# Preparing the next image six units before the last one ends, and the offset convolution in three parts

## The chip, the core and the metric

The program runs on one core of a Trainium2 chip. The metric is the device time of one execution in microseconds; the kernel before takes 4003.83 us (median of 3 runs, 3988.3 to 4007.59). It works on TensorE (PE), VectorE (DVE), ScalarE (ACT), GpSimd (POOL) and on DMA queues that SyncE (SP) and POOL feed.

## The reference, cut to what matters

The input x is [32, 192, 32, 32]. Two residual blocks follow each other, image by image, except for the last normalization, whose statistics run over the whole batch:

```
x = x + attention(group_norm(x))            # channel attention, 4 matmul stages
x = x + deform_block(group_norm(x))

deform_block(v):
    offset = clip(conv3x3(v, off_w) + off_b, -8, 8)         # 18 channels: y and x shift of 9 taps
    mask   = 2 * sigmoid(conv3x3(v, mask_w) + mask_b)       # 9 channels
    y      = sum over taps of w_tap . bilinear(v, position + tap + offset) * mask  + proj_b
    yn     = (y - mean) * rsqrt(var + 1e-5) * gamma + beta  # mean, var over batch and pixels
    return gelu(yn)
```

The 27 channels of offset and mask are computed together: this is the *offset convolution*.

## The kernel before, in words

Each of the 32 images is 8 tiles of 128 pixels. The sampling is done with matmuls: `Z = x2 . w` is computed per chunk of 4 rows (`zps`, split in two halves of 16 bits each, `zh` and `zl`), and for each tile a sparse matrix S of interpolation weights is built, turned and split in the same way (`sT`, `sps`, `sh`, `sl`), and then y = sum S . Z (`acc`). An image is 48 **units**. The main work of unit u, in `part1`, is:

- PE: `turn_s(u+2)` (three transposes, L666), `convolve(u)` (nine matmuls, L683 to L685), `z_group(u+10)` (five matmuls, L652 to L656). For the last units, u+2 and u+10 reach into the next image.
- ACT: the 16-bit copies `sh` of unit u+2 (L905) and `zh` of unit u+10 (L871). In each sixth unit it also takes y out of `acc` (`ypm`, L927 and L928).
- DVE: the remainders `sl` (L1161) and `zl` (L1155) behind them.
- POOL: one product `sT` (L1343) of row weights `ay` and column weights `bx` for two units, in a ring of three. So product p waits until PE has turned unit 2(p-3)+1.

PE may turn s of unit u+2 and convolve unit u only when DVE has written `sl` of unit u.

Beside this, `part0(k)` prepares the next image in 48 **steps** k, one behind the main work of each unit, and on every engine in the program's order (there is no planner; each engine is a straight list of instructions with waits on semaphores). Before the change step k stands in unit k of the image ahead. The steps that matter here:

- k = 0 to 4: statistics of x for the first group norm (DVE L993 to L1012, PE L517), k = 6 to 9: ACT normalizes, k = 12 to 22: attention (PE), k = 23 to 26: its result is added, k = 28: second group norm.
- k = 30 to 33: ACT normalizes into `x2`. k = 32 to 36: DVE writes the remainder (L1018) and, in `move`, two shifted copies (L1024, L1025) and two seam copies (L1027, L1028) of each of three planes. The last one raises `x2_moved`.
- k = 38 and 39: PE does the offset convolution, 4 tiles of 27 matmuls in each step (L594). It waits for `x2_moved`.
- k = 40 to 46: DVE takes the offsets out of PSUM (L1115 to L1122), makes the row weights in two halves (L1126, mask L1135, product L1137, which raises `hats`), ACT applies Abs and Relu to them, POOL and ACT make the column weights `bx` in four parts (L1327, L862 and L864). The first part belongs to step 41. The other three belong to main units (POOL after products 1, 4 and 10; ACT in units 4, 16 and 28).

Some work is tied to the unit, not to the step: PE turns the finished y (`turn_y`, L696) in units 14, 26, 38 and at the end, DVE scales it (`scale_y`, L1223) in units 19, 31, 43 and at the end, and DVE takes statistics of y in units 38, 39 and, for the second half, in units 5 and 6 of the next image (L1233). `z_group(0)` of the next image stands in unit 38 and waits for `x2_moved`.

```
part1(0, 0, True)
with nc.Fori(1, NB - 2, 2, ...) as b:
    part1(b, 1, True)
    part1(b + 1, 0, True)
part1(NB - 1, (NB - 1) % 2, False)
```

Two images are one round of a loop; the first and the last image stand outside it. Before image 0 the 48 steps of its own preparation run alone. `where_far`, at the end of every image, is a branch that skips a rare long pass.

Of the kernel before, what the change touches and what calls it, by code (L numbers as in the profile page):

```python
# [43 lines left out]
TILES = N // P  # L44
# [5 lines left out]
WRAP = 3  # L50
KO = 3 * C
UNITS = 6 * TILES
HEAD_SCALE = float((C // 4) ** (-0.5))
GN_EPS = 1e-5
BN_EPS = 1e-5
# [27 lines left out]
def build(nc, x, w_qkT, w_v, w_outT, b_out, w_off, b_off, w_proj, proj_b, gamma, beta,  # L83
          avg, cy, cx, eye, out):
    NB = x.shape[0]
# [4 lines left out]
    with ExitStack() as ctx:  # L90
# [154 lines left out]
        s_lo = sem("s_lo")  # L245
# [29 lines left out]

        SLOTS = UNITS
        CONST_DMAS = 4
# [58 lines left out]
        def images(program, eng):  # L336

            part0, part1, weights_ready = program  # L340
            for u in range(SLOTS):
                part0(u, 0, 0)
                if u == 15:
                    weights_ready()
            part1(0, 0, True)
            with nc.Fori(1, NB - 2, 2, engines=bass.OrderedEngineSet([eng.engine]), hint_back_edge=True) as b:
                part1(b, 1, True)
                part1(b + 1, 0, True)
            part1(NB - 1, (NB - 1) % 2, False)


        far_bodies = []
# [146 lines left out]
        def _(pe):  # L499
# [106 lines left out]
            def part0(u, b, par):  # L606
# [22 lines left out]
                    apply_m(u - 23, b)  # L629
                if u == 28:  # L630
                    group_stats(1, b)
                if 38 <= u < 40:
                    for t in range(TILES // 2):
                        offset_conv(TILES // 2 * (u - 38) + t, b, par)

            def z_group(g, b, par):

# [60 lines left out]
                mm.then_inc(yt_ps, 1)  # L698

            def far_pass(b, par, more):  # L700
                pe.wait_ge(s_lo, UNITS * (b + 1) + 2 * more)
                pe.wait_ge(y_ch, 4 * (b + 1))
                pe.wait_ge(y_pm, TILES * (b + 1))

# [39 lines left out]
            def part1(b, par, more):  # L744
# [5 lines left out]
                for u in range(UNITS):  # L750
                    if u + 2 < UNITS:
                        turn_s(u + 2, b)
                    elif more:
                        turn_s(u + 2 - UNITS, b + 1)
                    convolve(u, b, par)
                    if u == 9:
                        offset_max(b)
                    if u == 20:
                        flag = is_far(pe, b, par)
                    if u + AHEAD < UNITS:  # L760
                        z_group(u + AHEAD, b, par)
                    elif more:
                        z_group(u + AHEAD - UNITS, b + 1, 1 - par)
                    if u % 12 == 2 and u > 12:
                        turn_y(u // 12 - 1, b)
                    if more:
                        part0(u, b + 1, 1 - par)
                turn_y(3, b)
                where_far(flag, pe, b, par, more, far_pass, (fz_ps, FAR_Z), (fs_ps, FAR_UNITS), (fsz_done, FAR_UNITS),
                          (fyt_ps, TILES))  # L770
# [7 lines left out]
        def _(act):  # L778
# [128 lines left out]
            def part1(b, par, more):  # L907
# [5 lines left out]
                for u in range(UNITS):  # L913
# [8 lines left out]
                    if u % 6 == 5:  # L922
                        t = u // 6
# [6 lines left out]
                        split_z(u + AHEAD, b, par)  # L930
                    elif more:
                        split_z(u + AHEAD - UNITS, b + 1, 1 - par)
                    if more:
                        part0(u, b + 1, 1 - par)
                where_far(flag, act, b, par, more, far_pass, (fz_hi, FAR_Z), (fs_hi, FAR_UNITS), (fy_pm, TILES))

            images((part0, part1, lambda: None), act)
# [16 lines left out]
        def _(dve):  # L954
# [282 lines left out]
            def part1(b, par, more):  # L1237
# [5 lines left out]
                for u in range(UNITS):  # L1243
# [17 lines left out]
                        y_stats(u - 38, b, par)  # L1261
                    if u % 12 == 7 and u > 12:
                        scale_y(u // 12 - 1, b, par)
                    if more:
                        part0(u, b + 1, 1 - par)
                scale_y(3, b, par)
                where_far(flag, dve, b, par, more, far_pass, (fz_lo, FAR_Z), (f_st, 3 * TILES), (fs_lo, FAR_UNITS),
                          (fy_ch, TILES))
# [29 lines left out]
        def _(pool):  # L1298
# [14 lines left out]
                pool.tensor_tensor(nbias[:, :], nbias[:, :], minus[:, :], ALU.mult).then_inc(gn_bias, 1)  # L1313

            def part0(u, b, par):
                if u == 5:
                    group_rstd(0, b)
                if u == 29:
                    group_rstd(1, b)
                if u == 41:  # L1320
                    column_distance(0, b, par)

            def column_distance(q, b, par):
# [7 lines left out]
            def part1(b, par, more):  # L1331
                for p in range(3 * TILES):
                    t, ky = tile_at(p // 3, par), p % 3
# [10 lines left out]
                        .then_inc(st_made, 1)  # L1344
                    if p in (1, 4, 10):
                        column_distance((1, 4, 10).index(p) + 1, b, par)
                    if more:

                        for u in (2 * p - 4, 2 * p - 3):
                            part0(u, b + 1, 1 - par)  # L1350

            images((part0, part1, lambda: None), pool)

# [56 lines left out]
```

## Time and profile before

| | |
|---|---|
| median of 3 runs | 4003.83 us |
| the profiled execution: its time, its span | 3993.97 us, 3992.2 us |
| PE, DVE, ACT, POOL busy | 89%, 66%, 53%, 35% of the span |
| mean granted TensorE clock | 0.968 of full speed |
| two images in the middle of the run (rows below) | 230.65 us, 115.3 us each |

The span has three parts: about 120 us in which image 0 is prepared, 32 images, and about 200 us at the end in which PE is idle and the batch normalization is applied to y as it comes back from memory. A timeline row gives start and duration in us, the engine, the line, what is written and read, the shapes, and in brackets how long the engine was idle just before and which instruction ended that.

### The profile page before, as it was taken

The page shows a single profiled execution, that of the slowest core. Times are in us where ns is not written, and L with a number is a line of the kernel's source. Part 1 is how long each engine was busy: PE and PEld are TensorE (multiplying, and loading weights), DVE is VectorE, ACT ScalarE, POOL GpSimd, SP SyncE. Part 2 cuts the span into 40 slices and gives each one's busy share as a digit, 9 for nine tenths or more (in the row PEclk, how much of TensorE's full clock was granted, in tenths as well). Part 3 has the DMA queues.
Part 4 walks back from the last instruction along what each step waited for, and adds up shares of the span by engine and source line. Part 5 has one row for each costly group of instructions (what it writes and reads, how often), then busy time and mean ns, then how long its engine had stood idle before and what let it go on. Part 6 is the DMA issues. An engine that isn't in the chain of part 4 may idle for free.

```text
span 3992.2 us, 110012 instructions
## 1 busy us (share of the span) xinstructions
PE 3544.1 (89%) x38338; PEld 3034.8 (76%) x38338; DVE 2646.4 (66%) x5834; ACT 2111.3 (53%) x4790; POOL 1412.8 (35%) x1165
## 2 busy tenths in 40 slices
PE   3999999999999999999999999999999999999700
PEld 2788887888888888888888888888888888888700
DVE  3577766676677667677766676677667667766522
ACT  1555555565555555555555565555555555555432
POOL 1333333343433333333333343333333333333311
PEclk8999999999999999999999999999999999999955
DMA  2000000000000010000000000000000001000299
GB/s 63 20 10 28 28 27 22 28 28 19 20 28 28 20 28 28 28 10 28 28 20 28 28 28 15 23 28 28 20 28 28 28 10 28 28 20 18 76 377 322
DMA packets 50722, 170.05 MB, mean 43 GB/s; under 512 B 9664, under 2 KB 10880, under 8 KB 50176
## 3 DMA queue, kind: packets, MB, share of 16 engines
q1 hardware_dynamic: 39584, 136.75, 11.2%
q0 software_dynamic: 7168, 25.17, 1.6%
q8 instruction: 337, 5.52, 0.6%
q14 instruction: 209, 1.71, 0.1%
q10 hardware_dynamic: 3424, 0.90, 0.1%
HBM read 87.29 MB, written 75.50 MB: 41 GB/s over the span
## 4 chain that ended last, share of the span: by engine, by line
PE 66%; DVE 12%; issue 9%; DMA 4%; POOL 3%; ACT 3%; DVEq 1%; SPq 1%; ACTq 0%; POOLq 0%
PE sps L666 10%; PE acc L683 6%; PE acc L685 6%; PE acc L684 6%; PE l L594 4%; PE zps L652 3%; PE zps L656 3%; PE zps L653 3%; PE zps L655 3%; PE zps L654 3%; DVE zl L1155 3%; DMA xn<-x_scratch 2%; POOL sT L1343 2%; DVE sl L1161 2%; PE l L526 2%
## 5 line engine op out<-in xcount | busy, mean ns | idle before, releaser
L1343 POOL TENSOR_TENSOR sT<-ay,bx 128x768 f32<-128x768 f32 x768 | 1149.5, 1507 | 1363.4 <-PE sps L666 1292.5
L1161 DVE TENSOR_TENSOR sl<-sps,sh 128x384 f16<-128x384 f32 x1536 | 846.0, 551 | 563.8 <-ACT sh L905 557.7
L683 PE MATMUL acc<-zh,sh 128*128 128x192 f16 x4608 | 1133.7, 246 | 0.9 <-issue 0.6
L685 PE MATMUL acc<-zh,sl 128*128 128x192 f16 x4608 | 1133.6, 246 | 0.0
L684 PE MATMUL acc<-zl,sh 128*128 128x192 f16 x4608 | 1133.6, 246 | 0.0
L905 ACT CAST sh<-sps 128x384 f16<-128x384 f32 x1536 | 741.7, 483 | 695.3 <-PE sps L666 689.6
L871 ACT CAST zh<-zps 128x288 f16<-128x288 f32 x1536 | 620.4, 404 | 638.8 <-PE zps L656 611.7
L1155 DVE TENSOR_TENSOR zl<-zps,zh 128x288 f16<-128x288 f32 x1536 | 693.2, 451 | 334.3 <-ACT zh L871 325.4
L666 PE MATMUL sps<-eye,sT 128*128 128x128 f32 x4608 | 785.8, 279 | 127.2 <-DVE sl L1161 99.4
L666 PEld LDWEIGHTS sps<-eye,sT 128*128 128x128 f32 x4608 | 530.9, 140 | 283.5 <-DVE sl L1161 167.9
L684 PEld LDWEIGHTS acc<-zl,sh 128*128 128x128 f16 x4608 | 450.9, 98 | 17.7 <-issue 0.8
L683 PEld LDWEIGHTS acc<-zh,sh 128*128 128x128 f16 x4608 | 450.8, 98 | 2.4 <-DVE sl L1161 0.5
L685 PEld LDWEIGHTS acc<-zh,sl 128*128 128x128 f16 x4608 | 450.9, 98 | 0.0
L652 PE MATMUL zps<-wpr_h,x_hi_a 128*128 128x288 f16 x1344 | 384.6, 286 | 1.0 <-DVE zl L1155 0.6
L653 PE MATMUL zps<-wpr_l,x_hi_a 128*128 128x288 f16 x1344 | 384.4, 286 | 0.0
L654 PE MATMUL zps<-wpr_h,x_lo_a 128*128 128x288 f16 x1344 | 384.4, 286 | 0.0
L655 PE MATMUL zps<-wpr_h,x_hilo_b 128*128 128x288 f16 x1344 | 384.4, 286 | 0.0
L656 PE MATMUL zps<-wpr_l,x_hilo_b 128*128 128x288 f16 x1344 | 384.4, 286 | 0.0
L1327 POOL TENSOR_TENSOR bx<-off,cx_sb 128x576 f32<-128x576 f32 x128 | 155.5, 1215 | 459.0 <-DVE off L1122 459.0
L1309 POOL TENSOR_TENSOR rstd<-gvar,mhalf 128x2 f32<-128x2 f32 x64 | 44.9, 702 | 553.9 <-DVE gvar L1012 553.9
L594 PE MATMUL l<-wof,x2s_hi_a 128*128 128x54 f16 x1536 | 182.8, 186 | 9.8 <-DVE x2w_hilo_b L1028 9.8
L594 PE MATMUL l<-wof,x2s_lo_a 128*128 128x54 f16 x1536 | 182.6, 186 | 0.0
(200 smaller groups left out, 6482.7 us busy)
## 6 DMA issues: line engine op xcount, KB each, us to landing
xin<-in_x SPq DMA_DIRECT2D x32, 512.0 KB, 5.4
xin<-in_x SPq DMA_DIRECT2D x64, 256.0 KB, 6.0
x_scratch<-x SPq DMA_DIRECT2D x32, 512.0 KB, 2.7
y_scratch<-ych SPq DMA_DIRECT2D x32, 512.0 KB, 2.7
zh<-y_scratch SPq DMA_DIRECT2D x20, 512.0 KB, 11.1
zl<-x_scratch SPq DMA_DIRECT2D x20, 512.0 KB, 12.5
out<-zh POOLq DMA_DIRECT2D x20, 512.0 KB, 8.6
x_scratch<-x SPq DMA_DIRECT2D x32, 256.0 KB, 3.4
```

The lines of the kernel that those rows point to most:

```text
L594: mm = pe.matmul(o, src[:, row * W:(row + ROWS_T) * W], wof[:, m, k].rearrange("p i j -> p (i j)"), start=(k == 0 and n == 0), stop=(k == ...
L652: pe.matmul(o, at(0), wpr_h[:, 0, ky, n], start=True, stop=False)
L653: pe.matmul(o, at(0), wpr_l[:, 0, ky, n], start=False, stop=False)
L666: mm = pe.transpose(sps[u % 2][:, kx * P:(kx + 1) * P], sT[:, g, kx, c * P:(c + 1) * P], eye32[:, :])
L683: pe.matmul(acc[:, 0:C], s_h, zh[:, j, ky, z], start=start and kx == 0, stop=False)
L684: pe.matmul(acc[:, 0:C], s_h, zl[:, j, ky, z], start=False, stop=False)
L685: mm = pe.matmul(acc[:, 0:C], s_l, zh[:, j, ky, z], start=False, stop=stop and kx == 2)
L871: act.copy(z_piece(zh, g, par), zps[:, g % 2, 0:KO // 2]).then_inc(z_hi, 1)
L905: act.copy(sh[:, u % S_RING].rearrange("p k n -> p (k n)"), sps[u % 2][:, 0:3 * P]).then_inc(s_hi, 1)
L1155: dve.tensor_tensor(z_piece(zl, g, par), zps[:, g % 2, 0:KO // 2], z_piece(zh, g, par), ALU.subtract)\
L1161: dve.tensor_tensor(one(sl), sps[u % 2][:, 0:3 * P], one(sh), ALU.subtract).then_inc(s_lo, 1)
L1343: pool.tensor_tensor(sT[:, p % ST_RING].rearrange("p k (r x) -> p k r x", r=R), a, x_, ALU.mult)\
```

## The change

Every engine's step k + 6 now stands in unit k. In units 42 to 47 of image b stand steps 0 to 5 of image b + 2, since steps 6 to 47 of image b + 1 are done by then. Before image 0 these six steps of image 1 run too. Three images instead of one are written out behind the loop. On POOL the numbers of the steps change (5, 29, 41 become 9, 33, 45) because its loop over products now asks for units 2p and 2p+1 instead of 2p-4 and 2p-3; the same operations move by the same six units, three products. The offset convolution is done in steps 37, 38 and 39 with 2, 3 and 3 tiles.

```
+SHIFT = 6
...
+            for u in range(SHIFT):
+                part0(u, 1, 1)
+            part1(0, 0, 2)
+            with nc.Fori(1, NB - 4, 2, engines=bass.OrderedEngineSet([eng.engine]), hint_back_edge=True) as b:
+                part1(b, 1, 2)
+                part1(b + 1, 0, 2)
+            for b in range(NB - 3, NB):
+                part1(b, b % 2, min(2, NB - 1 - b))
+
+        def prepare(part0, u, b, par, more):
+
+            if u + SHIFT < SLOTS:
+                if more:
+                    part0(u + SHIFT, b + 1, 1 - par)
+            elif more == 2:
+                part0(u + SHIFT - SLOTS, b + 2, par)
...
-                if 38 <= u < 40:
-                    for t in range(TILES // 2):
-                        offset_conv(TILES // 2 * (u - 38) + t, b, par)
+                if 37 <= u < 40:
+                    for t in ((0, 1), (2, 3, 4), (5, 6, 7))[u - 37]:
+                        offset_conv(t, b, par)
...
-                    if more:
-                        part0(u, b + 1, 1 - par)
+                    prepare(part0, u, b, par, more)
...
-                    if more:
-
-                        for u in (2 * p - 4, 2 * p - 3):
-                            part0(u, b + 1, 1 - par)
+                    for u in (2 * p, 2 * p + 1):
+                        prepare(part0, u, b, par, more)
```

The change moves instructions in three places that the prediction speaks of. The first is PE where the offset convolution begins. Before, it stands in unit 38, behind a z product that itself waits for `x2_moved`, and behind the turn of y:

```order
L652 MATMUL zps<-wpr_h,x_hi_a 128x288 [waits z_lo,x2_moved]
L653 MATMUL zps<-wpr_l,x_hi_a 128x288
L654 MATMUL zps<-wpr_h,x_lo_a 128x288
L655 MATMUL zps<-wpr_h,x_hilo_b 128x288
L656 MATMUL zps<-wpr_l,x_hilo_b 128x288
L696 MATMUL yt<-eye,ypm 128x128 [waits y_ch,y_pm]
L697 MATMUL yt<-eye,ypm 128x128
L696 MATMUL yt<-eye,ypm 128x128
L697 MATMUL yt<-eye,ypm 128x128
L594 MATMUL l_1<-wof,x2s_hi_a 128x54 [waits x2_moved]
```

With the change it begins one step earlier, directly behind the z product of that unit (the lines of the new file are higher by some):

```order
L697 MATMUL acc<-zh,sl 128x192
L664 MATMUL zps<-wpr_h,x_hi_a 128x288 [waits z_lo]
L665 MATMUL zps<-wpr_l,x_hi_a 128x288
L666 MATMUL zps<-wpr_h,x_lo_a 128x288
L667 MATMUL zps<-wpr_h,x_hilo_b 128x288
L668 MATMUL zps<-wpr_l,x_hilo_b 128x288
L606 MATMUL l_1<-wof,x2s_hi_a 128x54 [waits x2_moved]
```

The z product ahead no longer waits for `x2_moved`, and the turn of y has gone from there to another step.

The second place is DVE behind the first half of the row weights (mask and product). Before:

```order
L1135 TENSOR_SCALAR mask<-mask 128x72
L1137 TENSOR_TENSOR ay<-ay,mask 128x288
L1159 ISA
L1161 TENSOR_TENSOR sl<-sps,sh 128x384 [waits s_hi]
L1154 ISA
L1155 TENSOR_TENSOR zl<-zps,zh 128x288 [waits z_hi]
L1218 ISA
L1223 TENSOR_SCALAR ych<-yt,unscale,pb 128x256 [waits yt_ps]
```

With the change:

```order
L1145 TENSOR_SCALAR mask<-mask 128x72
L1147 TENSOR_TENSOR ay<-ay,mask 128x288
L1169 ISA
L1171 TENSOR_TENSOR sl<-sps,sh 128x384 [waits s_hi]
L1164 ISA
L1165 TENSOR_TENSOR zl<-zps,zh 128x288 [waits z_hi]
L1169 ISA
L1171 TENSOR_TENSOR sl<-sps,sh 128x384 [waits s_hi]
L1164 ISA
L1165 TENSOR_TENSOR zl<-zps,zh 128x288 [waits z_hi]
```

The scaling of y, tied to unit 43, no longer follows; it stands six steps later.

The third place is POOL behind the first part of the column weights. Before, one product follows, then comes the end of the image, and the next product waits for `hats`:

```order
L1327 TENSOR_TENSOR bx<-off,cx_sb 128x576 [waits off_sb]
L1343 TENSOR_TENSOR sT<-ay,bx 128x768 [waits s_ps]
L346 UNCONDITIONAL_BRANCH
L346 BRANCH_PREFETCH_HINT
L346 ISA
L1337 ISA [waits hats]
L1339 ISA [waits bx_made]
```

With the change:

```order
L1336 TENSOR_TENSOR bx<-off,cx_sb 128x576 [waits off_sb]
L1352 TENSOR_TENSOR sT<-ay,bx 128x768 [waits s_ps] x4
L349 UNCONDITIONAL_BRANCH
L349 BRANCH_PREFETCH_HINT
L349 ISA
L1346 ISA [waits hats]
```

Four products of the running image, which need no new weights, now stand between them.

## Rows read from the trace of the kernel before

**Rows 1.** Busy time in a stretch of two images: length, PE, PEld, DVE, ACT, POOL, clock, DMA.

```profile
1711.22:1941.87 230.65, 220.72 (x2403) 189.22 (x2400) 160.98 (x360) 128.02 (x296) 85.35 (x68) 1.00 0.09 25
```

**Rows 2.** Waits of PE: engine, line, waited for; us in total, times, longest.

```profile
PE sps L666 <- DVE sl L1161: 99.4, 126, 1.2
...
PE l L594 <- DVE x2w_hilo_b L1028: 9.8, 1, 9.8
```

**Rows 3.** Timeline of PE, units 37 (1705.70), 38 (1708.67), 39 (1713.78) and 40.

```profile
1705.70 0.55 PE L666 MATMUL sps<-eye,sT 128*128 128x128 f32 x3 [0.31 <-DVE sl L1161]
...
1708.67 0.55 PE L666 MATMUL sps<-eye,sT 128*128 128x128 f32 x3 [1.07 <-DVE sl L1161]
...
1710.62 0.27 PE L696 MATMUL yt<-eye,ypm 128*128 128x128 f32 x1
...
1711.05 0.19 PE L594 MATMUL l<-wof,x2s_hi_a 128*128 128x54 f16 x1
...
1713.78 0.53 PE L666 MATMUL sps<-eye,sT 128*128 128x128 f32 x3
...
1718.23 0.53 PE L666 MATMUL sps<-eye,sT 128*128 128x128 f32 x3
```

**Rows 4.** The chain that ended last, the half of the offset convolution in unit 38.

```profile
1711.22 2.72 PE l L594 x108
```

**Rows 5.** Timeline of DVE, steps 32 to 36 of the same image.

```profile
1698.28 1.71 DVE L1018 TENSOR_TENSOR x_lo_a<-xn,x_hi_a 128x1024 f16<-128x1024 f32 x1
...
1701.43 1.45 DVE L1027 COPY x2w_hi_a<-x_hi_a 128x96 f16<-128x96 f16 x1
...
1706.61 1.45 DVE L1027 COPY x2w_lo_a<-x_lo_a 128x96 f16<-128x96 f16 x1
...
1708.07 0.54 DVE L1161 TENSOR_TENSOR sl<-sps,sh 128x384 f16<-128x384 f32 x1
...
1709.68 0.17 DVE L1028 COPY x2w_hilo_b<-x_hilo_b 128x96 f16<-128x96 f16 x1
```

**Rows 6.** Timeline of POOL, the same image and the beginning of the next.

```profile
1706.33 1.69 POOL L1343 TENSOR_TENSOR sT<-ay,bx 128x768 f32<-128x768 f32 x1 [3.49 <-PE sps L666]
1722.30 1.16 POOL L1327 TENSOR_TENSOR bx<-off,cx_sb 128x576 f32<-128x576 f32 x1 [14.28 <-DVE off L1122]
1723.41 1.69 POOL L1343 TENSOR_TENSOR sT<-ay,bx 128x768 f32<-128x768 f32 x1
1727.03 2.92 POOL L1343 TENSOR_TENSOR sT<-ay,bx 128x768 f32<-128x768 f32 x2 [1.93 <-DVE ay L1137]
```

**Rows 7.** Timeline of PE, the starts of units 44 and 45.

```profile
1725.77 0.55 PE L666 MATMUL sps<-eye,sT 128*128 128x128 f32 x3 [0.61 <-DVE sl L1161]
...
1727.78 0.55 PE L666 MATMUL sps<-eye,sT 128*128 128x128 f32 x3
```

**Rows 8.** Line L1075, a tensor-scalar operation: count; duration ns least/median/most; forms.

```profile
L1075 DVE TENSOR_SCALAR gram<-gram,rinv x64: 303/313/831, 66.6 to 3626.7; 128x192 f32<-128x192 f32 x32, 64x192 f32<-64x192 f32 x32
```

**Rows 9.** Timeline of DVE and ACT: remainder of step 10, column weights of unit 4.

```profile
1755.82 1.70 DVE L1018 TENSOR_TENSOR xhl_b<-xn,xhl_b 64x1024 f16<-64x1024 f32 x1
...
1742.04 0.69 ACT L862 ACTIVATE bx<-bx 128x576 f32<-128x576 f32 x1
```

**Rows 10.** Timeline of DVE, steps 41 to 46 (row weights).

```profile
1722.96 0.81 DVE L1126 TENSOR_TENSOR ay<-off,cy_sb 128x288 f32<-128x288 f32 x1
...
1726.04 0.19 DVE L1135 TENSOR_SCALAR mask<-mask 128x72 f32<-128x72 f32 x1
...
1726.30 0.46 DVE L1137 TENSOR_TENSOR ay<-ay,mask 128x288 f32<-128x288 f32 x1
1727.16 0.56 DVE L1161 TENSOR_TENSOR sl<-sps,sh 128x384 f16<-128x384 f32 x1 [0.40 <-ACT sh L905]
...
1732.69 1.79 DVE L1137 TENSOR_TENSOR ay<-ay,mask 128x288 f32<-128x288 f32 x1
```

**Rows 11.** Timeline of DVE, step 2: statistics of half of x.

```profile
1740.37 1.27 DVE L993 BATCH_NORM_STATS2 stats<-xin 128x6 f32<-128x512 f32 x2
```

More of the change, by code:

```diff
@@ L344, in images @@
                     weights_ready()
[L345 to L349, printed above, removed]
+            for u in range(SHIFT):
[12 more added lines that the diff above has]
+                part0(u + SHIFT - SLOTS, b + 2, par)
         far_bodies = []
@@ L700, in far_pass @@
             def far_pass(b, par, more):
-                pe.wait_ge(s_lo, UNITS * (b + 1) + 2 * more)
+                pe.wait_ge(s_lo, UNITS * (b + 1) + 2 * (more > 0))
                 pe.wait_ge(y_ch, 4 * (b + 1))
@@ L1263, in part1 @@
                         scale_y(u // 12 - 1, b, par)
-                    if more:
-                        part0(u, b + 1, 1 - par)
+                    prepare(part0, u, b, par, more)
                 scale_y(3, b, par)
@@ L1315, in part0 @@
             def part0(u, b, par):
-                if u == 5:
+                if u == 9:
                     group_rstd(0, b)
-                if u == 29:
+                if u == 33:
                     group_rstd(1, b)
-                if u == 41:
+                if u == 45:
                     column_distance(0, b, par)
@@ L1346, in part1 @@
                         column_distance((1, 4, 10).index(p) + 1, b, par)
-                    if more:
-                        for u in (2 * p - 4, 2 * p - 3):
-                            part0(u, b + 1, 1 - par)
+                    for u in (2 * p, 2 * p + 1):
+                        prepare(part0, u, b, par, more)
             images((part0, part1, lambda: None), pool)
```

## The prediction, made before the changed kernel ran

> **What bounds the kernel now.** I read the busy shares first, then the waits of PE, then a stretch of two images, then the timelines of the four engines in one image. PE is busy for 220.72 us of the 230.65 us of two images, at full clock (2.4 GHz, granted 1.00), while DVE, ACT and POOL have 161, 128 and 85 us of work there [rows 1]. So PE is the bound, and what can be won is in its waits. The largest named one is for `sl`, the remainder that DVE writes: 99.4 us in total, about 3 us an image. PE has waited long for `x2_moved` at the offset convolution only once, before image 0 [rows 2].
>
> The timeline of PE shows where this lies [rows 3]. Half an offset convolution takes 2.72 us [rows 4], and unit 39 with its half takes 1718.23 - 1713.78 = 4.45 us, so a bare unit is about 1.73 us. Unit 37 began at 1705.70 and should have ended at 1707.43, but unit 38 begins at 1708.67: 1.24 us lost. DVE explains it: in steps 32 to 36 it has two remainders and three moves beside its two operations a unit, and the `sl` that unit 38 needs ends only at 1708.07 + 0.54 = 1708.61 [rows 5, 3]. The seam copies there take 1.45 us each, where the last one of the same size takes 0.17 us. The reason is in the timeline of POOL: a product `sT` began at 1706.33 and ended at 1708.02, just around the copy at 1706.61 to 1708.06 [rows 5, 6]. DVE waits while POOL has the memory port. This matters for everything below. PE's start of a unit frees POOL's ring in every second unit, so these meetings repeat from image to image, and a shift by an even number of units keeps which units they are.
>
> After the offset convolution there is a second soft place: unit 44 begins 0.61 us late, behind `sl` again, while the row and column weights are made [rows 7].
>
> **The change part by part.** It removes and adds no arithmetic. All costs are of order, and I follow one image in the clock of the trace. k is the step of the preparation; it now stands in unit k - 6.
>
> *First part of the offset convolution, step 37.* The DVE list up to `x2_moved` is the same except that the scaling of y ahead of it is gone, and that is no gain, since the next `sl` had to wait for ACT (four normalizations of steps 30 to 33) anyway. So `x2_moved` comes at 1709.68 + 0.17 = 1709.85 as now [rows 5]. PE arrives at 1707.43. It must now wait 2.5 us until about 1709.95, where it waited 1.24 us. Behind this wait stand its own next turn of s and z product, and so ACT and DVE, too. Then come 54 matmuls, 2.72 x 54/108 = 1.36 us [rows 4]; then unit 38 (1.70) with 81 matmuls (2.04), unit 39 the same: 1709.95 + 1.36 + 2 x 3.75 = 1718.8, against 1718.23 now [rows 3]. The present 4.77 us of other work between includes 0.43 us for the turn of y (1710.62 to 1711.05 [rows 3]), which goes to step 44. I take **+0.6 us an image**. Bounds: -0.4 (if `x2_moved` comes 1 us earlier because the scaling is gone) and +1.0.
>
> *Turns of y.* They go from steps 14, 26, 38 to 20, 32, 44, 0.43 us each. Step 14 to 20 is even: PE's extra at step 20 also moves POOL's next product, which blocks the softmax scaling (0.83 us instead of 0.31 [rows 8]) that PE waits for. Step 26 to 32: it moves the end of POOL's product, for which the remainder of step 32 (1.71 us, a wait in it [rows 5]) stands still, and saves about 0.33 at step 26. **+0.1**; bounds -0.4 and +0.4.
>
> *Column weights of unit 4* now meet step 10, right behind ACT's four normalizations: twice 0.69 = 1.4 us [rows 9] ahead of `zh`. DVE's remainder of step 10, which begins at 1755.82 now, begins about 1 us later but then, I estimate, misses POOL's product and is up to 0.5 us shorter than its 1.70. PE has about that much slack. **+0.35**; bounds 0 and +1.4.
>
> *Row weights, steps 41 to 46.* Here the port decides. POOL has products ready to run when the column weights are made at 1722.30 and a product at 1723.41 to 1725.10; then it waits until 1727.03 for `hats`, that is for DVE's product L1137 [rows 6]. In this gap DVE runs the mask operation (1726.04, 0.19) and the product (1726.30, 0.46) undisturbed [rows 10]. With the change POOL does not wait: three further products of the running image follow, from 1725.10 to 1726.58 and to 1728.06 (1.48 each, half of 2.92 or a little more [rows 6]). A tensor-scalar operation like the mask does wait for POOL: L1075, of the same kind, has 0.31 us as its median and 0.83 us at most [rows 8]. So the mask operation waits until 1726.58; POOL then takes the port for the next product, and L1137 waits until about 1728.15, as its second half does now with 1.79 us [rows 10]. The `sl` that now starts at 1727.16 starts at about 1728.5, and ends at 1729.1. PE needs it at its start of unit 45, now 1727.78 [rows 7]. **+1.3**; bounds +0.1 (the turn of y alone, in the place of the old 0.33 wait) and +1.5. Two statements of the Trainium skill bear on it (SBUF — State Buffer, § Who interferes with whom): the shared port is an exclusive lock held for the whole instruction, and `tensor_scalar` in its two-port modes takes it. That agrees with 1.45 against 0.17 us; no run here shows the mask operation itself meeting a product. Were the mask operation free of the lock, L1137 would ask first at 1726.58 and the term would be 0.3, not 1.3.
>
> *Later.* DVE's scaling of y lands in step 49 beside statistics of x; the group matmuls of step 52 may wait for it. **+0.15**; bounds 0 and +0.9, all of one scaling. The waits of the last turn of y and of the branch at the image's end stay, only beside other steps.
>
> *Loads.* SP loads the next x when step 26 is done, now in unit 20; it is read in unit 42. 22 units of 1.7 us or more are over 37 us for 0.8 MB: hidden. Were it late, DVE's statistics and all behind them would wait for it. SP's stores of y stand behind it, unchanged.
>
> *Before image 0,* DVE makes four statistics of image 1 (twice 1.27 us [rows 11]) and the short moments, and PE waits for them ahead of all its z products. With group matmuls about **+4.5 us once**; bounds 2.5 and 7. For the two further images that are written out instead of looped I find no cost: their lists are the same, and image 0 was written out before, too.
>
> **Sum.** 0.6 + 0.1 + 0.35 + 1.3 + 0.15 = 2.5 us for each of 31 preparations = 78 us, and 4.5 us: 82 us. The profiled execution took 3993.97 us (its span 3992.2 us and 1.8 around it); that gives 4076 us. The median of the runs, 4003.83, lies 10 us above this execution; the measurement of this kernel tells about 0.5%, 20 us, from no change.
>
> **The rivals.**
>
> *A. No meeting on the port.* The row weights slip in between products, everything else as above: 0.6 + 0.1 + 0.35 + 0.1 + 0.1 = 1.25 us, times 31, plus 4.5: 4037 us. For it speaks that the times differ by tenths (1726.30 against 1726.58), against it that POOL has two products back to back there.
>
> *B. The waits cancel.* PE's later arrival gives DVE and ACT time that the replay undercounts, and the shift's terms vanish; the start remains: 3998 us. For it speaks that PE's idle time is only 5 us an image and that every term is a small one.
>
> *C. Faster: `x2_moved` comes in time.* The two seam copies lose 1.28 us each to POOL's products. If the products leave them alone, `x2_moved` comes 2.6 us earlier, at 1707.3, before PE ends unit 37. Then the waits before units 37 and 38 (0.31 and 1.24 us) and the z product's 0.3 us vanish, and step 37's 54 matmuls start at once: -1.8 us; with the row weights in the present order and a wait of 0.6 before unit 44 gone as well, -2.4 us. Times 31, plus 4.5 us: 3924 us. It decides when the product starts over 0.3 us later against the copy than now (1706.33 against 1706.61 [rows 5, 6]). Against it: both starts hang on the same start of a PE unit. If only one copy is freed, 1.3 us an image go against the +1.25 of A, near 3998 again.
>
> *D. The first part does nothing.* If other work fills the 1.24 us at step 38 as before and step 37's wait is absorbed, the split changes nothing and only the shift counts: 1.9 us an image, 4057 us. This lies within the forecast's range.
>
> **How the numbers follow.** Chances: forecast with D 0.42; A 0.22; B 0.14; C 0.12, and 0.10 for milder gains between B and C. Above 4024 lies slower by over 0.5%: the forecast and A, 0.63 with what the bounds leave (4037 is not far from the limit). Same has 0.15, faster 0.22, from B, C and what lies between. The range reaches from 3972, leaving out C in full, to 4105: the upper bounds of all terms would add 75 us, which will not all hold together; I take 30. About a fifth is left out.
>
> **What would show it.** Right: a wait of about 2.5 us at the first offset matmul in each image, on L1028's successor; the mask product of the first half at 1.5 us or more; two images at 235 us instead of 230.65; the wait for `sl` before unit 38 gone. Wrong: no wait there, seam copies of 0.17 us in all three planes, or two images at 230 us or less. If the wait is there but two images take 233 us, A holds.

## The result, and the profile after

The changed kernel took 4152.51 us (median of 4 runs, 4142.17 to 4163.03), the kernel before 4002.81 us beside it: ratio 1.038, with an interval of 1.0342 to 1.0419. The forecast was 4076 us and slower, with a range to 4105. So the direction was right, and the loss of 150 us is nearly twice the 82 that the sum gave. The profiled execution took 4156.31 us (span 4154.6).

The page's line of busy time: PE is busy for 86% of the span, where it was 89%, DVE for 65% (66% before) and ACT for 50% (53%). PE's loss is idle time and slower matmuls, not work.

```profile
PE 3589.5 (86%) x38338; PEld 3062.5 (74%) x38338; DVE 2681.3 (65%) x5834; ACT 2095.8 (50%) x4790; POOL 1400.0 (34%) x1165
```

The waits of PE, as in [rows 2] (us in total, times, longest):

```profile
PE l L606 <- DVE x2w_hilo_b L1038: 81.3, 32, 9.8
PE sps L678 <- DVE sl L1171: 67.9, 95, 2.0
PE l L529 <- DVE mv L1012: 34.7, 33, 14.2
PE acc L695 <- ACT ypm L939: 29.8, 63, 0.8
PE l L550 <- DVE xhl_b L1028: 15.1, 29, 9.5
```

The wait for `x2_moved` at the first offset matmul, which stood only ahead of image 0, is now there 32 times: (81.3 - 9.8) / 31 = 2.31 us an image. The wait for `sl` fell from 99.4 to 67.9 us, since one of its four places in an image has gone. Three waits are new in every image. Those for `ypm` and `xhl_b` stand in one unit, shown below (9.5 of the 15.1 us for `xhl_b` fall once, before image 0). The one for `mv`, statistics that DVE takes, was there twice before, 17.1 us in total, and is now there 33 times: about 0.57 us an image, at step 52. Steps 48 to 53 are here steps 0 to 5 of the image after.

Stretches of the changed kernel (length, PE, PEld, DVE, ACT, POOL, clock, DMA): the first covers two images, the others are 6.8 us long and begin at the start of the new wait, in two different images:

```profile
1769.64:2007.99 238.35, 223.01 (x2403) 190.51 (x2399) 163.14 (x360) 127.07 (x296) 84.53 (x68) 0.99 0.08 24
```

```profile
1756.93:1763.73 6.80, 4.50 (x71) 4.33 (x72) 4.53 (x13) 0.88 (x2) 0.41 (x1) 0.75 0.01 2
...
1996.78:2003.58 6.80, 4.50 (x127) 4.37 (x128) 4.99 (x14) 1.27 (x3) 0.40 (x1) 1.00 0.01 2
```

Two images take 238.35 us instead of 230.65, with the same matmuls. And something stands here that the prediction did not have: in these stretches the granted clock is 0.75 to 0.77 on average in 20 of the 31 images and 1.00 in the other 11. A mean of 0.75 means that half of the stretch ran at the lower of the two levels, 1.2 instead of 2.4 GHz. In the stretch at 0.75 71 matmuls are done, in the one at full clock 127. The price can be read within this one kernel: steps 37 and 38 together take 10.88 us in the 20 images and 9.35 us in the 11. That is 1.53 us for each, and 20 x 1.53 = 31 us over the run.

The timeline of PE in the first of these images, steps 37 to 39:

```profile
1755.02 0.55 PE L678 MATMUL sps<-eye,sT 128*128 128x128 f32 x3 [0.78 <-DVE sl L1171]
...
1759.23 0.23 PE L606 MATMUL l<-wof,x2s_hi_a 128*128 128x54 f16 x1 [2.31 <-DVE x2w_hilo_b L1038]
...
1761.66 0.88 PE L678 MATMUL sps<-eye,sT 128*128 128x128 f32 x3
...
1763.82 0.19 PE L606 MATMUL l<-wof,x2s_hi_a 128*128 128x54 f16 x1
...
1765.87 0.53 PE L678 MATMUL sps<-eye,sT 128*128 128x128 f32 x3
```

Behind the wait the offset matmuls start about 45 ns apart (1759.23 to 1761.66 for 54), in the next unit about 25 ns (1763.82 to 1765.87 for 81): step 37 takes 1761.66 - 1755.02 = 6.64 us, where in an image at full clock it takes 5.58.

The timeline of DVE ahead of that wait answers to [rows 5]:

```profile
1747.51 2.15 DVE L1028 TENSOR_TENSOR x_lo_a<-xn,x_hi_a 128x1024 f16<-128x1024 f32 x1
...
1751.11 0.17 DVE L1037 COPY x2w_hi_a<-x_hi_a 128x96 f16<-128x96 f16 x1
...
1752.46 1.92 DVE L1028 TENSOR_TENSOR x_hilo_b<-xn,x_hilo_b 64x1024 f16<-64x1024 f32 x1
...
1755.93 1.45 DVE L1037 COPY x2w_lo_a<-x_lo_a 128x96 f16<-128x96 f16 x1
...
1759.00 0.17 DVE L1038 COPY x2w_hilo_b<-x_hilo_b 128x96 f16<-128x96 f16 x1
```

The first seam copy is free now (0.17 instead of 1.45, so 1.28 us less), but both remainders lost to products of POOL instead: 2.15 us against 1.71, and 1.92 us against the 1.22 of the kernel before:

```profile
1703.83 1.22 DVE L1018 TENSOR_TENSOR x_hilo_b<-xn,x_hilo_b 64x1024 f16<-64x1024 f32 x1
```

That is 1.14 us more, and the second copy still takes 1.45. So `x2_moved` comes as late as the prediction said: 1759.17 - 1755.02 = 4.15 us behind the start of step 37, as before (1709.85 - 1705.70).

The second new place is the unit with step 12. Its timelines of ACT, DVE and PE:

```profile
1806.00 1.29 ACT L806 ACTIVATE xhl_b<-xin,nbias,rstd 128x1024 f16<-128x1024 f32 x1
...
1807.50 0.74 ACT L873 ACTIVATE bx<-bx 128x576 f32<-128x576 f32 x1
1808.31 0.68 ACT L875 ACTIVATE bx<-bx 128x576 f32<-128x576 f32 x1
1808.90 0.38 ACT L882 CAST zh<-zps 128x288 f16<-128x288 f32 x1
```

```profile
1809.31 0.46 DVE L1165 TENSOR_TENSOR zl<-zps,zh 128x288 f16<-128x288 f32 x1 [1.06 <-ACT zh L882]
1809.80 1.93 DVE L1028 TENSOR_TENSOR xhl_b<-xn,xhl_b 64x1024 f16<-64x1024 f32 x1
```

```profile
1808.89 0.49 PE L678 MATMUL sps<-eye,sT 128*128 128x128 f32 x3
1810.05 0.26 PE L695 MATMUL acc<-zh,sh 128*128 128x192 f16 x1 [0.67 <-ACT ypm L939]
...
1811.78 0.23 PE L550 MATMUL l<-eye,xh_a 128*128 128x128 f16 x1 [0.20 <-DVE xhl_b L1028]
...
1812.37 0.55 PE L678 MATMUL sps<-eye,sT 128*128 128x128 f32 x3
```

The column weights (`bx`) stand right behind the normalizations on ACT, `zh` and `ypm` come late, and DVE's remainder, which starts later, meets a product all the same (1.93 us, 1.70 before [rows 9]). The unit takes 1812.37 - 1808.89 = 3.48 us instead of 2.10.

The third place is step 44. POOL and DVE, against [rows 6, 10]:

```profile
1774.82 4.57 POOL L1352 TENSOR_TENSOR sT<-ay,bx 128x768 f32<-128x768 f32 x3
```

```profile
1777.44 0.56 DVE L1145 TENSOR_SCALAR mask<-mask 128x72 f32<-128x72 f32 x1
...
1778.08 1.63 DVE L1147 TENSOR_TENSOR ay<-ay,mask 128x288 f32<-128x288 f32 x1
```

Three products run back to back, to 1774.82 + 4.57 = 1779.39. The mask operation (0.19 us before) ends at the seam of the second and third, DVE's product (0.46 us before) only after the third.

**The balance by units.** These are differences of the mean length of each unit of PE over 31 images, before and after, by the step that it holds. A unit is taken from its first turn of s to that of the next. Steps 35 to 39 together +1.23 us; steps 9 to 15 without the turn of y +1.54 (step 12 alone +1.36); the turns in steps 14 to 32 +0.01; steps 43 and 44 +0.96; steps 47 to 53, with the image's end, +0.41; all others +0.06: 4.21 us. From the start of image 0 to that of the last one the run took 3704.9 us instead of 3574.3, and 130.6 / 31 is the same 4.21 us an image. Image 0 began 5.6 us later (124.9 against 119.3), and what comes from the start of the last image on took 324.8 instead of 298.6 us: 26.2 us that no term of the prediction held. The sum is 162.4 us, the difference of the spans.

### The profile page after: what moved, and what is told of

The parts are those of the page before. It is cut to its first block, busy times and chain, and to the rows that moved or that the text cites. A ratio compares the mean times of both kernels' runs of the same rounds, so it can differ in the third digit from the quotient of the medians.

```text
span 4154.6 us, 109071 instructions
## 1 busy us (share of the span) xinstructions
PE 3589.5 (86%) x38338; PEld 3062.5 (74%) x38338; DVE 2681.3 (65%) x5834; ACT 2095.8 (50%) x4790; POOL 1400.0 (34%) x1165
## 4 chain that ended last, share of the span: by engine, by line
PE 61%; DVE 12%; issue 12%; ACT 6%; DMA 4%; DVEq 2%; ACTq 2%; SPq 1%; POOL 0%; POOLq 0%
PE sps L678 10%; PE acc L695 6%; PE acc L696 6%; PE acc L697 6%; PE l L606 5%; PE zps L668 3%; PE zps L664 3%; PE zps L665 3%; PE zps L666 3%; PE zps L667 3%; DVE zl L1165 2%; DMA xn<-x_scratch 2%; ACT zh L882 2%; DVE sl L1171 2%; PE l L538 2%
## 5 line engine op out<-in xcount | busy, mean ns | idle before, releaser
L678 PE MATMUL sps<-eye,sT 128*128 128x128 f32 x4608 | 789.7, 281 | 99.6 <-DVE sl L1171 67.9
L606 PE MATMUL l<-wof,x2s_hi_a 128*128 128x54 f16 x1536 | 198.7, 191 | 81.3 <-DVE x2w_hilo_b L1038 81.3
L606 PEld LDWEIGHTS l<-wof,x2s_hi_a 128*128 128x128 f16 x1536 | 140.8, 99 | 92.4 <-DVE x2w_hilo_b L1038 90.8
```

What stands on the lines that cost most here:

```text
L606: mm = pe.matmul(o, src[:, row * W:(row + ROWS_T) * W], wof[:, m, k].rearrange("p i j -> p (i j)"), start=(k == 0 and n == 0), stop=(k == ...
L678: mm = pe.transpose(sps[u % 2][:, kx * P:(kx + 1) * P], sT[:, g, kx, c * P:(c + 1) * P], eye32[:, :])
```

## The experiments

Ten kernels ran. Medians of the kernel before beside them were 4001.96 us (the first four), 4005.37 (the next four) and 4006.52 (the last two). Each ratio is against the kernel before.

**1. The shift alone**: the changed kernel with the offset convolution back in two halves.

```
-                if 37 <= u < 40:
-                    for t in ((0, 1), (2, 3, 4), (5, 6, 7))[u - 37]:
-                        offset_conv(t, b, par)
+                if 38 <= u < 40:
+                    for t in range(TILES // 2):
+                        offset_conv(TILES // 2 * (u - 38) + t, b, par)
```

> The changed kernel, but with the offset convolution again in steps 38 and 39 with four tiles each: the shift by six units alone. The traces of before and after, laid over each other step by step, give an image 115.5 and 119.5 us; of the 4 us, 1.4 arise at step 12, about 1.4 at steps 35 to 39 (less 0.43 for the turn of y that has left), 1.1 at step 44, 0.5 at step 52 and 0.25 at the image's end. Theory S (a sum of separate meetings): only the part at steps 35 to 39 goes, about 1.2 us an image with the slow clock of TensorE behind the 2.3 us wait: 4152 - 37 = 4115 us, step 12 still 1.4 us long. Theory W (one wait, and all else follows from it): with the wait gone nearly everything comes back, 4010 us.

4090.16 us, 1.0219 (1.0198 to 1.024). The shift costs 88 us by itself, and the three parts on top of it 62, 25 us more than the expectation had (4115 us). Its waits of PE:

```profile
PE sps L678 <- DVE sl L1171: 101.5, 126, 2.0
PE l L529 <- DVE mv L1012: 34.8, 33, 14.2
PE acc L695 <- ACT ypm L939: 30.1, 63, 0.8
```

The waits for `ypm` and `mv` are the shift's, the one of 2.31 us is not there. Steps 12 (3.47 us) and 44 (3.04) are as in the changed kernel.

**2. The three parts alone**, in the kernel before (the same lines the other way round).

> The kernel before with only the offset convolution changed: two, three and three tiles in steps 37, 38 and 39, no shift. Theory S: PE waits 2.3 us for x2_moved in step 37 instead of 1.24 us ahead of step 38, and in many images the clock falls to its lower level for some us: 1.0 to 2.0 us an image, 4035 to 4065 us; all other steps as before. Theory W: the whole loss of the change, over 4120 us. If the split is good by itself and only the shift spoils it: 3985 us or less.

4053.31 us, 1.0121 (1.0097 to 1.0144), as expected. Only three units differ: step 37 takes 5.85 us (2.98 before), 38 4.74 (5.10), 39 3.77 (4.45): +1.8 us an image. The wait is the one of the changed kernel:

```profile
PE l L594 <- DVE x2w_hilo_b L1028: 81.4, 32, 9.8
```

The low clock follows it in 16 of the 31 images. So both parts of the change cost time, and they nearly add up: 51 + 88 = 139 against 150 us.

**3. The column weights two units later**, in the changed kernel.

```
-                    if u % 12 == 4 and u < 36:
+                    if u % 12 == 6 and u < 36:
```

> The changed kernel, but ScalarE makes the second to fourth part of the column weights in units 6, 18 and 30 instead of 4, 16 and 28, that is in steps 12, 24 and 36 and no longer right behind the four normalizations. Theory S: the 1.4 us at step 12 go, 31 x 1.4 = 43 us, 4109 us; a few tenths may come back at step 35, since GpSimd's product there is no longer late and meets the seam copy again. Rival (the 1.4 us come from the statistics of y that now stand in steps 11 and 12, not from the column weights): step 12 stays at 3.5 us and the time within 10 us of 4152.

4141.06 us, 1.0343 (1.0322 to 1.0364). The expectation had 4109. Half of it came as expected: step 12 is back at 2.02 us. But the wait at step 37 grew to (121.1 - 9.8) / 31 = 3.6 us:

```profile
PE l L606 <- DVE x2w_hilo_b L1038: 121.1, 32, 9.8
```

Step 37 takes 7.38 us instead of 6.11 and step 38 4.94 instead of 4.23, while step 36 is 0.93 us shorter; the low clock now follows the wait in 27 of the 31 images. The column weights move in all three of their units, and those of unit 28 (step 34) set when POOL's product starts, and so which of DVE's operations meet it. Moved, they release two products at once, and beside the seam copy of DVE (1.45 us, as in the changed kernel) a shifted copy meets one too (1.72 us instead of 0.44):

```profile
1869.31 3.15 POOL L1352 TENSOR_TENSOR sT<-ay,bx 128x768 f32<-128x768 f32 x2 [5.96 <-ACT bx L875]
```

```profile
1869.41 1.72 DVE L1035 COPY x2s_lo_a<-x_lo_a 128x992 f16<-128x992 f16 x1
1871.05 1.45 DVE L1037 COPY x2w_lo_a<-x_lo_a 128x96 f16<-128x96 f16 x1
```

The expectation reckoned with a few tenths there; for the most part the gain of step 12 was lost again. That the weights cause step 12's loss is shown; that they can be moved alone is not so.

**4. POOL held back at the row weights**, in the changed kernel, so that it waits for the mask product as before:

```
+                    if p == 21 and more:
+                        pool.wait_ge(hats, 2 * (b + 1) + 1)
```

> The changed kernel with one wait more: GpSimd makes its product 21 of the running image only when the first half of the new row weights is done, as it did before the change. This keeps the memory port free for VectorE's mask and product in step 42. Theory S (the port): unit 38, which is step 44, falls by 0.6 us, since L1147 takes 0.46 instead of 1.63 us: 31 x 0.65 = 20 us, 4132 us. Rival (the 0.6 us at step 44 come from the turn of y and the statistics on VectorE): no change there, 4152 us, or slower because product 21 is late for PE.

4120.93 us, 1.0309 (1.028 to 1.0337). DVE's row weights, this kernel:

```profile
1770.79 0.19 DVE L1145 TENSOR_SCALAR mask<-mask 128x72 f32<-128x72 f32 x1
1771.05 0.46 DVE L1147 TENSOR_TENSOR ay<-ay,mask 128x288 f32<-128x288 f32 x1
```

Mask and product are undisturbed, and step 44 takes 2.17 us instead of 3.04. That is the meeting on the port, taken away without touching DVE's own list: 0.87 x 31 = 27 us. The time behind the last image fell too, from 239.35 to 214.2 us; that goes with the length of POOL's list, see 7. Against it, steps 37 and 38 took 0.24 us an image more (the low clock followed the wait in 24 images, not 20), and image 0 began 2 us later. That makes 27 + 25 - 7 - 2 = 43 us; the span of the profiled execution fell by 44 us (4154.6 to 4110.4), the median by 32.

**5. A shift of 12**, with the convolution in halves.

```
-SHIFT = 6
+SHIFT = 12
```

> The changed kernel with a shift of twelve units instead of six, and the offset convolution in steps 38 and 39 with four tiles each. The work tied to units recurs every twelve units (turn and scaling of y, column weights on ScalarE in units 4, 16, 28), so it meets the same steps of the preparation as before the change, except at the ends of its lists. Theory S (the loss lies in which step meets which unit): steps 12, 36 and 44 are as before the change, an image takes about 116 us instead of 117.2, and with some 8 us more before image 0 the time is 4010 to 4045 us. Rival (a preparation that runs ahead over the image's end costs by itself, and more so the longer it is): 4100 us or more.

4066.76 us, 1.0157 (1.013 to 1.0183): a miss, outside the expectation. Step 12 takes 2.13 us, nearly as before, so that loss belongs to where the column weights fall, as in 3. But step 44 still takes 3.04 us, which I had not expected: at a shift of 12, too, POOL does not wait for the row weights, and DVE's product L1147 takes 1.62 us for their first half. The unit count of the shift matters less than whether POOL waits.

**6. The seam copies on ACT**, in the kernel before. The first two of three planes:

```
+                if u in (35, 36):
...
+                    act.copy(seam[:, 0:WRAP], src[:, H - WRAP:H])
+                    ins = act.copy(seam[:, WRAP:2 * WRAP], src[:, 0:WRAP])
...
+                if k == 2:
                     seam = rows(x2w[k][:, par])
                     dve.tensor_copy(seam[:, 0:WRAP], src[:, H - WRAP:H])
```

ACT waits for the plane (a drain, and `xn_lo`), signals once with a semaphore of its own, and PE waits for that ahead of the first z product.

> The kernel before the change, but the seam copies of the first two planes are made by ScalarE in steps 35 and 36 instead of by VectorE in 33 and 35, where each waited 1.28 us for the memory port. PE waits for them at the first z product of the next image. Port theory: VectorE ends its moves 2.6 us earlier, the waits of PE before units 37 and 38 shrink by 1 to 2 us an image, 3940 to 3970 us. Rival (the meeting only moves to the next copy or remainder on the port, or ScalarE's four copies make sh late instead): 3990 to 4010 us.

3943.86 us, 0.9838 (0.9816 to 0.9861): 62 us faster than the kernel before, and the best of all. A seam copy in its timeline of ACT, and the wait of PE:

```profile
1679.01 0.27 ACT L856 COPY x2w_lo_a<-x_lo_a 128x96 f16<-128x96 f16 x1
```

```profile
PE sps L668 <- DVE sl L1176: 37.2, 64, 2.9
```

The wait for `sl` is 37.2 us instead of 99.4 [rows 2], 62 us less, and the 31 images together are 62 us shorter: steps 35 and 37 by 1.24 us each, while others are 0.5 us longer in all. (In the profiled execution the last image and the end took 17 us longer; why is open.) Four copies taken off DVE do it. DVE's queue was late because two of them met POOL; ACT makes each in 0.27 us. In this kernel none of ACT's copies runs beside a product, so by itself it does not show that ACT is free of the meeting. Kernel 10 does.

**7. POOL's instruction list 16 longer**, in the changed kernel: behind the last image, ahead of the normalization, the lines

```
+            for i in range(16):
+                pool.memset(padt[:, i:i + 1], -1.0)
```

> The changed kernel with sixteen tiny memsets more on GpSimd behind its last image. In the changed kernel the part behind the last image took 239 us against 212 before the change and 214 in e4, and GpSimd's first store of the output was issued 13 us after its sum was ready, at a time when the DMA engines are full and instructions are being fetched. Theory (GpSimd's last code is fetched then, and where the piece that is missing begins hangs on the number of its instructions): with another length the part falls to about 214 us and the time to 4128 us. Rival (the state of the memory, or the shift itself): 239 us and 4152 us. e1, with the same GpSimd list as the changed kernel, had 239 us.

4139.41 us, 1.0333 (1.0313 to 1.0354), between the expectation's 4128 and its rival's 4152: 13 us less than the changed kernel with 16 instructions more (the profiled span 17 us less). From the first table load of ACT behind the last image to the end it took 220.7 us instead of 239.35 (211.6 in the kernel before). POOL's timeline there, first of the changed kernel, then of this one:

```profile
3936.11 1.30 POOL L1369 DMA_DIRECT2D out<-xin  x2 [22.09 <-DVE zh L1300]
```

```profile
3925.98 0.76 POOL L1372 DMA_DIRECT2D out<-xin  x1 [10.68 <-DVE xin L1301]
```

and DVE's sums and ACT in the changed kernel:

```profile
3922.00 1.23 DVE L1300 TENSOR_TENSOR xin<-xin,x 128x1024 f32<-128x1024 f32 x1 [6.94 <-ACT xin L956]
```

```profile
3971.69 2.37 ACT L956 ACTIVATE xin<-xin,gb,ga 128x1024 f32<-128x1024 f32 x2 [24.47 <-DMA xn<-x_scratch]
```

The sum that the store needs is there at 3922.00 + 1.23 = 3923.23, but POOL issues it only at 3936.11, 12.9 us later, and behind it ACT stands idle 24.47 us for a load. With the longer list the store follows its sum after 0.8 us. The long end is there in the changed kernel and in 1, 3, 5 and 10 (237 to 241 us), which all have the same number of POOL instructions ahead of that store (2210 in the trace); it is missing in 2, 4, 6, 7, 8 and 9, where the number is another (214 to 223). The profile also lists packets of instructions among the DMA queues. While the store is late, from 3923.3 to 3936.2, the changed kernel's queues read (packets, MB, share of 16 engines):

```profile
q1 hardware_dynamic: 1082, 3.82, 103.9%
q14 instruction: 2, 0.02, 0.4%
```

The last packet of instructions starts at 3934.2, 1.9 us before the store. In 1, 3, 5 and 10 such a packet starts 1.9 us before the late store too; in the six kernels without the long end none comes in the 4 us before it.

**8. The shift with both places mended** (1, 3 and 4 together).

> The shift by six units with all three named meetings taken away at once: offset convolution in steps 38 and 39, column weights on ScalarE in units 6, 18, 30, product 21 of GpSimd held until the first row weights are done. Theory S (separate meetings that add up): of the 4 us an image of the changed kernel only 0.5 at step 52 and 0.3 at the image's end stay, 31 x 0.8 + 6 = 31 us, 4033 us, and 4058 if the last part is the slow one. Rival (taking one away makes another, as step 37 did in e3): 4070 us or more.

4034.75 us, 1.008 (1.0061 to 1.0098), where 4033 was expected. So 0.8% is left: 116.0 us an image in the mean, against 115.2 before. The number came out by luck in part, since the expectation knew nothing of the clock: a wait for `sl` of 2.35 us stands ahead of the unit with step 38 in every image, and behind it the clock falls in 17 of the 31. These take 1.6 us more in steps 37 and 38, 27 us in all. Without that the kernel would be about level with the one before. One stretch at full clock and one with the fall:

```profile
1712.00:1720.00 8.00, 6.57 (x157) 6.30 (x158) 5.73 (x15) 1.54 (x4) 0.78 (x1) 1.00 0.01 2
1826.90:1834.90 8.00, 6.68 (x131) 6.08 (x132) 5.16 (x14) 0.88 (x2) 0.67 (x1) 0.79 0.01 2
```

**9. The three parts with the seams on ACT** (2 and 6).

> Kernel e6 (seam copies of the first two planes made by ACT) with the offset convolution in three parts from step 37, no shift. Theory S: the three parts are dear because step 37 comes before x2_moved is there; with the seam copies gone from DVE that signal comes about 1.3 us earlier, so PE waits some 1.0 to 1.7 us there instead of 2.3, too short to bring the clock down: 3965 to 3985 us, slower than e6 (3944), and less added than the 51 us that the parts added to the kernel before (4002 to 4053). Rival W: the split itself is dear (54 matmuls in three steps break the rhythm of PE and ACT), whatever x2_moved does: 3944 + 51 = 3995 us.

3977.91 us, 0.9932 (0.9908 to 0.9956), inside the expectation (3965 to 3985): the parts add 34 us to kernel 6, not 51, and stay a loss.

```profile
PE l L595 <- DVE x2w_hilo_b L1043: 49.7, 32, 9.6
```

The wait is (49.7 - 9.6) / 31 = 1.29 us an image. Even with `x2_moved` a microsecond earlier, step 37 comes too early for it.

**10. The changed kernel with the seams on ACT** (6's edit in it).

> The changed kernel with the seam copies of the first two planes made by ACT in its steps 35 and 36. Theory S: of the changed kernel's loss the wait at step 37 (2.3 us) and the slower clock behind it come from x2_moved being late; DVE is relieved of about 1.6 us of seam copies (1.45 and 0.17), so the wait falls below 1 us, the clock stays at its upper level, and the image becomes 2 to 3 us shorter: 4070 to 4095 us. The column weights at step 12, the row weights at step 44 and the slow end behind the last image stay. Rival W: another operation of DVE (the remainder, which collides with a product of POOL) simply slips and x2_moved comes as late as now: 4140 us or more.

4093.55 us, 1.0228 (1.02 to 1.0256): 59 us less than the changed kernel, inside the expectation, though the wait did not fall below 1 us: it is 1.29 us here too. A stretch from its start:

```profile
1734.30:1741.10 6.80, 5.51 (x156) 5.36 (x156) 3.99 (x10) 1.28 (x3) 0.43 (x1) 1.00 0.01 4
```

The clock stays at 2.4 GHz here and behind the waits of all other images. By the units, steps 37 and 38 took 8.33 us instead of 10.34, 2.00 us less: the wait gives 1.02 of it, and what is left, 0.98 us an image or 30 us, agrees with the 31 us read within the changed kernel.

This kernel also shows that ACT is free of the meeting: in 28 images a copy of ACT runs beside a product of POOL, nearly from its start to its end, and takes 0.27 us as elsewhere, where DVE's took 1.45.

```profile
1730.43 0.27 ACT L867 COPY x2w_hi_a<-x_hi_a 128x96 f16<-128x96 f16 x1
```

```profile
1729.21 1.48 POOL L1367 TENSOR_TENSOR sT<-ay,bx 128x768 f32<-128x768 f32 x1 [3.23 <-ACT bx L889]
```

## Why the prediction was right and wrong

Its mechanisms were mostly right and two of its sizes were not; two losses it did not have. Term by term, us an image:

| term | forecast | seen |
|---|---|---|
| steps 35 to 39, net | +0.6 | +1.23, of it 1.0 clock |
| turns of y | +0.1 | +0.01 |
| column weights (9 to 15) | +0.35 | +1.54 |
| row weights (43, 44) | +1.3 | +0.96 |
| later (47 to 53) | +0.15 | +0.41 |
| before image 0, once | +4.5 | +5.6 |
| behind the last image, once | 0 | +26 |

*First part of the offset convolution.* "It must now wait 2.5 us" was right: 2.31. That `x2_moved` would come no earlier was right as well, for another reason than given: not the same operations met POOL's products, but others for as long. Without the clock the term is +0.24, where the forecast had +0.6. **What failed is that the wait was priced as its length alone.** Behind it the granted clock fell to the lower of its two levels in 20 of 31 images, for 1.53 us each. Kernel 10 shows it from the other side: with a wait of 1.29 us it does not fall. The 31 us are two fifths of the 76 us by which the time lies above the forecast. That the split itself is to blame, and not the shift, is shown by 1 and 2. D, by which the first part would do nothing, is refuted: it costs 62 us on the shift and 51 alone.

*Column weights.* The second failed step, and the largest in size (1.54 - 0.35 = 1.19 us an image, 37 us), is "PE has about that much slack" and with it the value +0.35 between bounds of 0 and 1.4. The loss was 1.36 us at step 12, about the upper bound: 1.4 us of ACT work arrived at PE nearly whole. The remainder was guessed to start late and miss POOL's product; it started late and met it. The value was taken near the lower bound because of that guess; between such bounds, the row of ACT's 1.4 us was the nearer. Kernels 3, 5 and 8 give step 12 back when the weights move elsewhere.

*Row weights.* The mechanism was right in each of its steps: the mask operation waits for the second product (0.56 instead of 0.19) and the product for the third (1.63 instead of 0.46). The Trainium skill's page on SBUF (SBUF — State Buffer, § Who interferes with whom) says that a tensor-scalar operation in its two-port modes takes the shared port pair, and that whoever has the pair blocks the other for the whole instruction. The rows of the mask operation (0.56 us beside a product, 0.19 in kernel 4) agree. The reading by which the mask operation is free of it would have given +0.3, and falls. Rival A, with +0.1 here and 4037 us in all, falls with it.

*Later.* The group matmuls of step 52 do wait, for `mv`, as the prediction held possible; with 0.41 the term stayed within its bounds (0 and 0.9).

*Behind the last image.* The prediction said of the further images "their lists are the same" and gave them nothing; it looked at the work and not at the instructions' length or place. It was 26 us, a third of the excess. Kernel 7 takes 19 us of it away by POOL's list alone (239.35 to 220.7 us).

*B and C.* The waits did not cancel, and `x2_moved` did not come early. C's idea, that the seam copies are what is in the way, holds: only that an even shift does not free them. Kernel 6 frees them without the shift and gains 62 us, where C had 31 x 2.4 = 74.

*The range* ended at 4105, after "I take 30" of 75 us of upper bounds. Added up, the distances to the bounds are 0.4 + 0.3 + 1.05 + 0.2 + 0.75 = 2.7 us an image, and with the 2.5 us at the start 86 us, not 75, so that all of them together end at 4162. The clock and the end, together 57 us, were outside all of the terms; what else there was kept within its bounds or, with the column weights, just passed them (1.54 against 1.4). The "present 4.77 us of other work" in the first term does not come out of its rows (1718.23 - 1708.67 - 2 x 2.72 = 4.12); the +0.6 does not use it.

## What to carry to other kernels

Before moving work earlier, list what else the moved operation lands beside: here it was ACT's list (1.4 us whole) and which operation of DVE meets a product of POOL. Copies that were late because two engines met on a port gained 62 us here when a third engine made them; the shift, which moved work in time, only changed which operations met. And a wait of 2.3 us on PE in a steady stream of matmuls should be priced with a chance of the lower clock behind it, here another 1.5 us in two images of three.

## What the runs showed of the hardware that was not expected

- The clock fell after a wait of 2.31 us in 20 of 31 images (24 in kernel 4, 16 in kernel 2), after 2.35 us in kernel 8 in 17, after 3.6 us in kernel 3 in 27, and after 1.29 us in none of the 62 images of kernels 9 and 10. Why some images escape is open: the rows ahead of the waits read alike. In the changed kernel the fall comes at another place in each image, from 0.3 us before the end of the wait to 1.2 us behind it, though the wait is 2.30 or 2.31 us every time. The Trainium skill (TensorE: Matmul & The Clock Gate, Part 1: The HAM clock gate) says that the chip judges TensorE's activity on a count that runs freely of the kernel. By that rule the same wait could be met at different points of the count and fall on either side, which fits 20 of 31 and the moving place of the fall; no run here moved a wait on purpose to try it.
- The first output store of POOL came 12.9 us after its data in the changed kernel, and 0.8 us after it when POOL's list was 16 instructions longer. The DMA engines are fully taken in this time (103.9% for the data queue), and in all five kernels with the late store the last packet of instructions starts 1.9 us before it, so a late fetch of POOL's instructions fits well. It stays an inference: the profile does not say which engine's instructions a packet holds, and no run changed the load on the DMA engines. Shown is that the length of the list decides.
- DVE gets in between two products of POOL that run back to back: a mask operation that takes 0.19 us alone took 0.56 and ended at the seam of two.

Open is the rest of kernel 5 (why step 44 did not get better at a shift of 12 was read, not tried). Not tried either is moving the seam copies in time on DVE, against moving them to ACT. A kernel with 6 as its base and a better place for the row weights was not tried.
